# Two Swin blocks in one kernel: new orders of work on all five queues, a new ring of PSUM banks, and a semaphore step in place of a one-column product

## The reference

```
h = layernorm(x) * g + b                      # A0 / A1 in the kernel
h = roll(h, (-3, -3)); cut into windows of 7 x 7 = 49 tokens
q, k, v = h @ Wqkv + bqkv                     # first block 4 heads of 24, second 12 heads of 8
a = softmax(q * scale @ k.T + relative_bias[head] + shift_mask[window])
o = (a @ v) @ Wproj + bproj; windows back, rolled back
x = x + o
m = gelu(layernorm(x) @ W1 + b1)              # M0 / M1; hidden width 384
first block only: m = layernorm(m) * g3 + b3
x = x + m @ W2 + b2
```

## Time and profile before

| | us |
|---|---|
| median of 3 runs | 6845.63 |
| profiled execution, whole | 6848.46 |
| profiled execution, span from first to last instruction | 6846.5 |
| PE busy | 6637.3 (97%) |
| DVE busy | 5211.6 (76%) |
| ACT busy | 5460.3 (80%) |
| GpSimd (POOL) busy | 4494.8 (66%) |

### The profile page before, as it was taken

One profiled execution on the slowest core, in us unless ns is written; L12 is line 12 of the kernel. 1 busy time (PEld: TensorE's weight loads), 2 busy tenths in 40 slices (PEclk: granted clock), 3 DMA queues, 4 the chain that ended last, 5 costly groups with the idle time before them and its releaser, 6 DMA issues.

```text
span 6846.5 us, 283694 instructions
## 1 busy us (share of the span) xinstructions
PE 6637.3 (97%) x97324; PEld 5821.8 (85%) x97324; DVE 5211.6 (76%) x18725; ACT 5460.3 (80%) x11268; POOL 4494.8 (66%) x4612
## 2 busy tenths in 40 slices
PE   6999999999999999999999999999999999999998
PEld 5888888888888888888888888888888888888887
DVE  5777777777777777777777777777777777777775
ACT  4888888888888888888888888888888888888886
POOL 3666666666666666666666666666666666666664
PEclk8999999999999999999999999999999999999998
DMA  2111111111111111111111111111111111111111
GB/s 63 47 50 45 50 46 49 47 49 47 49 48 48 48 47 48 47 49 47 50 46 50 46 50 45 50 45 50 46 50 47 49 47 49 47 48 48 48 48 34
DMA packets 604527, 327.79 MB, mean 48 GB/s; under 512 B 449916, under 2 KB 603902, under 8 KB 604094
## 3 DMA queue, kind: packets, MB, share of 16 engines
q1 hardware_dynamic: 603992, 322.32, 18.2%
q10 hardware_dynamic: 486, 4.82, 0.2%
HBM read 82.89 MB, written 38.54 MB: 18 GB/s over the span
## 4 chain that ended last, share of the span: by engine, by line
PE 44%; SPq 39%; DMA 8%; issue 6%; ACT 2%; DVE 1%; POOL 0%; POOLq 0%; DVEq 0%; ACTq 0%
SPq L343 20%; PE ps L396 13%; SPq L331 10%; PE ps L486 10%; DMA vM<-vA 8%; PE ps L422 6%; PE ps L453 3%; SPq L321 3%; PE ps L510 3%; PE ps L432 3%; PE ps L414 3%; ACT kT L641 2%; SPq L313 2%; PE ps L523 2%; SPq L300 2%
## 5 line engine op out<-in xcount | busy, mean ns | idle before, releaser
L975 POOL TENSOR_TENSOR hid_sq<-hid 128x1176 f32<-128x1176 f32 x256 | 550.1, 2149 | 1443.2 <-ACT hid L696 1443.2
L679 ACT ACTIVATE probsT<-ps 98x392 f32<-98x392 f32 x2048 | 952.9, 492 | 498.9 <-PE ps L396 498.4
L848 DVE TENSOR_TENSOR shifted<-ps,negmax 113x392 f32<-113x392 f32 x2048 | 1161.3, 567 | 213.2 <-DVE negmax L844 0.5
L844 DVE TENSOR_REDUCE negmax<-ps 113x8 f32<-113x392 f32 x2048 | 1147.3, 560 | 208.8 <-PE ps L453 208.5
L396 PE MATMUL ps<-ident,probs 113*98 113x113 f32 x8192 | 1076.5, 264 | 9.5 <-ACT probs L672 5.8
L486 PE MATMUL ps<-vM,probsT 98*49 98x18 f32 (+1 forms) x32768 | 944.5, 202 | 134.1 <-DMA vM<-vA 132.4
L486 PEld LDWEIGHTS ps<-vM,probsT 98*49 98x49 f32 x32768 | 838.4, 125 | 272.6 <-issue 163.6
L672 ACT ACTIVATE probs<-shifted 113x392 f32<-113x392 f32 x2048 | 988.5, 518 | 9.8 <-DVE shifted L848 6.8
L664 ACT ACTIVATE ps<-table 113x392 f32 (+1 forms) x2048 | 956.4, 498 | 13.9 <-DVE y_out L880 2.6
L396 PEld LDWEIGHTS ps<-ident,probs 113*98 113x98 f32 x8192 | 801.0, 128 | 129.6 <-issue 81.1
L947 POOL TENSOR_TENSOR rstdA<-var_epsA,minus_half 98x4 f32<-98x4 f32 x512 | 517.4, 1011 | 576.5 <-DVE var_epsA L827 576.3
(11 more groups left out here) (98 smaller groups left out, 14713.8 us busy)
## 6 DMA issues: line engine op xcount, KB each, us to landing
kM<-kT SPq DMA_DIRECT2D x512, 85.8 KB
vM<-vA SPq DMA_DIRECT2D x1024, 41.3 KB
vM<-vA SPq DMA_DIRECT2D x1024, 38.3 KB
x_in<-in_x SPq DMA_DIRECT2D x256, 147.0 KB
x_again<-in_x SPq DMA_DIRECT2D x256, 147.0 KB
kM<-kT SPq DMA_DIRECT2D x1024, 36.8 KB
x_keep<-x_next SPq DMA_DIRECT2D x256, 147.0 KB
out_y<-y_out SPq DMA_DIRECT2D x256, 147.0 KB
```

What stands on the lines that cost most here:

```text
L679: act.activation(probsT[:, unit_buffer(L, u), :, :, :], free(ps[bank_of[f"T{L}{u}"]][0:PT, 0:1], (SP, 4), (64, 2), (1, TOK)), ACT.Copy).th ...
L844: dve.tensor_reduce(negmax[:, buf, :], s, AX.X, ALU.max, negate=True).then_inc(s_mx[L], 1)
L848: dve.tensor_tensor(shifted[0:SP, buf, :].rearrange("p (h k) -> p h k", k=TOK), s, free(negmax[:, buf, 0:1], (1, 8), (0, TOK)), ALU.add).t ...
```

## The change

All five orders, the lags and the banks are replaced, LAST goes from 5 to 6, and the one-column product becomes an increment of a new semaphore s_ready by PE's sequencer, which carries the same wait; nothing waits for s_ready. No other operation is added, removed or altered. The orders before are in the listing above; of the diff the new lines stand here.

```diff
-LAST = 5
+LAST = 6
...
+        s_ready = sem("s_ready")
...
+        BANKS = [("f1_1_1", 6, 0), ("k1", 4, 3), ("q1", 4, 1), ("xtM0", 3, 3), ("f1_2_1", 6, 0), ("v1", 4, 1),
+                 ("oT1", 5, 4), ("f1_0_0", 3, 3), ("f1_1_0", 3, 0), ("f1_2_0", 3, 4), ("pj1", 5, 1),
+                 ("xtA0", 1, 0), ("sc10", 4, 2), ("sc11", 4, 5), ("sc12", 4, 3), ("f2_1", 6, 1), ("T00", 2, 0),
+                 ("T01", 2, 4), ("f2_0", 3, 2), ("sc13", 4, 5), ("sc14", 4, 1), ("sc15", 4, 4), ("o0", 2, 7),
+                 ("T10", 4, 0), ("k0", 1, 3), ("T11", 4, 5), ("T12", 4, 0), ("q0", 1, 1), ("T13", 4, 3),
+                 ("oT0", 2, 5), ("v0", 1, 0), ("xtM1", 5, 3), ("pj0", 2, 2), ("o1", 4, 6), ("sc00", 1, 1),
+                 ("sc01", 1, 5), ("f1_0_1", 5, 0), ("xtA1", 3, 3), ("T14", 4, 4), ("T15", 4, 2)]
...
-                    pe.matmul(ps[bank_of["sc00"]][0:1, 0:1], ident[:, 1:2], ident[:, 0:1], start=False, stop=True, skip_group_check=True)
+                    pe.sem_inc(s_ready, 1)
```

More of the change, by code:

```diff
@@ L346, in body @@
             def body(i):
-                s0, s1, s2, s3, s5 = Strip(i, 0), Strip(i, 1), Strip(i, 2), Strip(i, 3), Strip(i, 5)
+                s0, s1, s4, s6 = Strip(i, 0), Strip(i, 1), Strip(i, 4), Strip(i, 6)
+                variants(s4, 1)
+                spread_v(s4, 1)
                 load(s0)
-                keep(s3)
+                store(s6)
+                keep(s4)
+                variants(s1, 0)
                 spread_v(s1, 0)
                 load_residual(s1)
[L352 to L355, removed]
             iterate(sp, body)
@@ L570, in body @@
[L570 to L598, removed]
+                s1, s2, s3, s4, s5, s6 = Strip(i, 1), Strip(i, 2), Strip(i, 3), Strip(i, 4), Strip(i, 5), Strip(i, 6)
@@ new lines, in body @@
+                fc1(s6, 1, 1)
+                k(s4, 1)
+                q(s4, 1)
+                attend(s5, 1, 4)
+                attend(s5, 1, 5)
+                xT(s3, "M0")
+                fc1(s6, 1, 2)
+                v(s4, 1)
+                o_turn(s5, 1)
+                fc1(s3, 0, 0)
+                fc1(s3, 0, 1)
+                fc1(s3, 0, 2)
+                project(s5, 1)
+                xT(s1, "A0")
+                scores(s4, 1, (0, 1, 2))
+                fc2(s6, 1)
+                probs_turn(s2, 0, 0)
@@ new lines, in body @@
+                probs_turn(s2, 0, 1)
+                fc2(s3, 0)
+                scores(s4, 1, (3, 4, 5))
+                attend(s2, 0, 0)
+                attend(s2, 0, 1)
+                probs_turn(s4, 1, 0)
+                k(s1, 0)
+                probs_turn(s4, 1, 1)
+                probs_turn(s4, 1, 2)
+                q(s1, 0)
+                probs_turn(s4, 1, 3)
+                o_turn(s2, 0)
+                v(s1, 0)
+                xT(s5, "M1")
+                project(s2, 0)
+                attend(s4, 1, 0)
@@ L600, in _ @@
+                attend(s4, 1, 1)
+                attend(s4, 1, 2)
+                attend(s4, 1, 3)
+                scores(s1, 0, (0, 1))
+                fc1(s5, 1, 0)
+                xT(s3, "A1")
+                probs_turn(s4, 1, 4)
+                probs_turn(s4, 1, 5)
             iterate(pe, body)
@@ new lines, in body @@
+                gelu(s6, 1, 0)
+                turned(s4, "A1")
+                probsT_out(s5, 1, 4)
+                probsT_out(s5, 1, 5)
+                seed(s4, 1, 0)
+                gelu(s6, 1, 1)
+                k_out(s4, 1)
+                q_out(s4, 1)
+                seed(s4, 1, 1)
+                turned(s3, "M0")
+                gelu(s6, 1, 2)
+                v_out(s4, 1)
+                o_out(s5, 1)
+                gelu(s3, 0, 0)
+                gelu(s3, 0, 1)
+                seed(s4, 1, 2)
@@ new lines, in body @@
+                gelu(s3, 0, 2)
+                exps(s2, 0, 0)
+                exps(s2, 0, 1)
+                turned(s1, "A0")
+                probsT_out(s2, 0, 0)
+                probsT_out(s2, 0, 1)
+                seed(s4, 1, 3)
+                exps(s4, 1, 0)
+                seed(s4, 1, 4)
+                seed(s4, 1, 5)
+                exps(s4, 1, 1)
+                exps(s4, 1, 2)
+                probsT_out(s4, 1, 0)
+                k_out(s1, 0)
+                exps(s4, 1, 3)
+                probsT_out(s4, 1, 1)
@@ L744, in _ @@
+                probsT_out(s4, 1, 2)
+                probsT_out(s4, 1, 3)
+                o_out(s2, 0)
+                exps(s4, 1, 4)
+                q_out(s1, 0)
+                turned(s5, "M1")
+                v_out(s1, 0)
+                seed(s1, 0, 0)
+                seed(s1, 0, 1)
+                exps(s4, 1, 5)
             iterate(act, body)
@@ L914, in body @@
             def body(i):
-                s0, s1, s2, s3, s4, s5 = Strip(i, 0), Strip(i, 1), Strip(i, 2), Strip(i, 3), Strip(i, 4), Strip(i, 5)
-                stats(s0, "A0")
[L917 to L936, removed]
+                s0, s1, s2, s3, s4, s5, s6 = Strip(i, 0), Strip(i, 1), Strip(i, 2), Strip(i, 3), Strip(i, 4), Strip(i, 5), Strip(i, 6)
+                normalise(s5, 1)
+                low_part(s3, 0)
+                residual(s5, 1)
+                shift(s4, 1, 0)
+                shift(s4, 1, 1)
+                finish1(s6)
+                shift(s4, 1, 2)
+                stats(s5, "M1")
+                third_stats(s3)
+                shift(s4, 1, 3)
+                shift(s4, 1, 4)
+                normalise(s2, 0)
+                finish0(s3)
+                stats(s3, "A1")
+                shift(s4, 1, 5)
+                residual(s2, 0)
+                low_part(s5, 1)
+                stats(s2, "M0")
+                shift(s1, 0, 0)
+                stats(s0, "A0")
+                shift(s1, 0, 1)
             iterate(dve, body)
```

64 lines of the change are left out of this document (11 added, 53 removed), and 6 rows, old and new, of the table BANKS.

## The result

The changed kernel took 6871.22 us (median of 7 runs, 6868.61 to 6876.12), the kernel before 6849.05 us beside it (7 runs, 6842.89 to 6854.27). The ratio is 1.0035 (95% interval 1.0026 to 1.0045): slower by 0.35%. I had predicted 6628 us, in a range of 6585 to 6740.

What follows compares the result with a forecast made beforehand. TensorE's own issue plus its wait for vM bounds the kernel; 26.22 - 0.73 - 0.06 - 0.16 + 0.10 = 25.37 us a strip, 0.85 less over 256 strips, gives 6628 us, 8-in-10 range 6585 to 6740.

Steps and rivals of the forecast that it cites:

- ACT's order: Turn of the loop: exps 5, table load, gelu and turned fit before k by 0.1 us plus the fc1.
- Rival 2: New wait replaces the old, likeliest at the loop's turn or sequencer's increment: 0.6 to 0.8 us a strip back; chance 0.10.
- vM, -0.73: SyncE's new order copies encoder 1's vM sooner, so TensorE's wait at L486 goes: -0.73 us a strip.
- The product of one column, -0.06: L445 on TensorE becomes a sequencer increment: -0.06 us a strip, between gain 0.12 and loss 0.09.
- Stretches, -0.16: TensorE has four stretches of small products a strip instead of five: -0.16 us, bounds -0.33 and +0.10.
- small waits, +0.10: Waits of the new order ending just before TensorE needs them; some come late: +0.10 us a strip (0 to 0.3).
- VectorE's order: L895 falls from 0.93 to 0.16 us, so q, reached at 3.59 us, does not wait for shift 4.
- rival 1: L895 stays at 0.93 us beside a GpSimd instruction and q waits 0.47 us: 6748 or 6723 us; chance 0.11.
- Rival 3: Ring through VectorE and the table load becomes the bound, slower than before, 6943 us at 26.6 a strip; chance 0.05.
- LAST = 6: Filling and emptying outside the ring: counted as 0 us, range -5 to +20 us.

Runs made afterwards that it cites:

- experiment 1: Changed kernel with gelu's two waits swapped (fc2's first, fc1's last): 6586.77 us, ratio 0.9622 to the kernel before.
- experiment 2: Changed kernel with gelu's two waits swapped only in the hardware loop, unrolled turns as they were: 6582.24 us, ratio 0.9616 to the kernel before.
- experiment 3: Kernel before with a semaphore step on ACT in encoder 1, putting the table load behind fc1's wait: 7192.49 us, ratio 1.0508.
- experiment 6: Kernel before, encoder 1's vM copies earlier on SyncE: one call moved, 8314.94 us; instead encoder 0's vM copies taken from in front, 6832.18 us.
- experiment 8: Kernel before with encoder 0's vM copies moved behind encoder 1's and add_bias moved behind rstd_of_third: 6662.64 us; with s_ready increment for one-column product too: 6661.65 us.
- experiment 4: Changed kernel with gelu's waits swapped and the old one-column product in place of the increment: 6622.16 us, ratio 0.967 to the kernel before.
- experiment 5: Kernel before with only the one-column product replaced by the semaphore increment: 6846.19 us, ratio 0.9998.
- experiment 7: Kernel before with add_bias(s4, 1) moved behind rstd_of_third(s2) on GpSimd, away from L895: 6845.38 us, ratio 0.9998.

## Why the prediction was wrong

The sum of what the change does to TensorE was nearly right: I had 25.37 us a strip, the kernel after without its hole takes 25.15 (experiment 1). The prediction failed in one step, and a rival that I gave 0.10 names its place. By the periods measured: -0.75 for vM and L895 together, -0.13 for the product, -0.22 for the rest of the order and +1.18 for the table load make +0.08 (26.25 to 26.33). The first of these was measured in the old order. I had -0.73, -0.06, -0.06 and nothing for the load.

**The step that failed** is ACT's order: "It fits, by 0.1 us plus the fc1, if exps 5 was done in time." Two things were wrong in it. First, it counted the load as done whenever the exponential is done and put nothing for it behind fc1; in the head of the loop the load waits for fc1, 1.60 us after the exponential is done, and that costs 1.18 us a strip (experiments 1 and 2; 3 shows the like in the other order). Secondly, it asked whether ACT is ready for k, while the first that wants ACT is fc1(s6, 1, 1), which takes gelu's bank, as the list of banks in the diff shows. This second point is the smaller: with another bank fc1 could have begun 0.92 us earlier and k have been wanted at 3025.54, but the copy turned(s4, "A1") ends only at 3026.14, so by these rows about 0.6 us would have stayed (an estimate; no run tried it). From the end of fc1(s5, 1, 0) TensorE has three turns to do, ACT the load of 1.28 us and gelu of 0.59. With the load out of the way the turns cover it, and ACT is even 0.23 us idle before gelu; with the load in it TensorE stands for 0.92 us, and the turns with the hole grow by 1.15. The kernel's text doesn't name the load; the trace does, and in the timeline before it could be seen that the load ran beside its fc1 and so that its place matters.

**Rival 2** had "most likely at the turn of the loop, where the branch, the table load and k meet", at 0.6 to 0.8 us a strip. The place was right, the price too low by a third to a half: 1.15 to 1.18. I priced it as margins overrun, not as a whole load of 1.28 moved onto the path.

**vM, -0.73.** The wait is gone, and its price was right as a price on TensorE (48 products now 1.21 us). But alone it is worth 0.07 (experiment 6); only with L895's fall is it worth 0.75 (experiment 8). The prediction took the whole -0.73 for the vM wait alone, and had L895's fall for another reason, so that the sum came out near is in part luck. It had the chain (q waits if L895 stays), in the new order; that the kernel before is bound by the same chain 0.07 us behind its vM wait I had not looked for.

**The product of one column, -0.06.** In the new order it is 0.13 (experiment 4), about the gain of 0.12 that I had as one bound: the increment hides wholly. In the old order it is 0 (experiment 5).

**Stretches, -0.16, and small waits, +0.10.** From the kernel before with its two chains mended (25.50) to the new order mended (25.15) it is 0.35 us; less the product's 0.13 the new order itself gives 0.22, where I had 0.06. How that divides between fewer stretches and waits that are no longer there, such as the one for low_part, was not tried.

**VectorE's order** came out as predicted: q doesn't wait (it starts 3.56 us after scores(s4, 1, (3, 4, 5)), from 3013.76 to 3017.32, where I had 3.59), and L896 is at 0.16. Here the Trainium skill (SBUF — State Buffer, section Who interferes with whom), by which any GpSimd instruction that reads SBUF shuts a VectorE instruction with two SBUF inputs out, would hold L896 until inverse_root ends, and so at 0.27 us in the row shown, and L895 of experiment 7 at 0.9. The trace agrees with that rule under the addition over 384 columns (0.93 us beside 1.00) and disagrees under inverse_root with four columns (0.16 beside 1.02, in all 252 runs of experiment 7 that start beside it); the measurement decides, and rival 1 was rightly priced low.

**Rival 3** didn't come: in the traces of the new order TensorE has no steady wait for VectorE. **LAST = 6**: outside the ring the kernel after spends 133 us, before 127, so +6, within what I gave; with the load in its place it is 140 to 148.

**The range** of 6585 to 6740 left out the whole of rival 2 and of anything slower. It would have held the time of the kernel with the load in its place (6587, and 6582 in its best form, just below). Most of the margins that I called small held; what moved the result was an instruction that I had not placed.

## What to carry to other kernels

When an order is turned so that another operation comes first in a loop's body, look at the instructions of the queue there and not at the text: a wait can sit on a register instruction, and an inserted table load then stands behind it. There is no one right order of the waits in the text: in the head of this loop fc1's wait had to be written last, in the unrolled turns first. So look, in each place, at which wait the load stands behind; here two waits swapped were worth 284 us of 6871. And where a wait that bounds a kernel is taken away, add up the second-longest chain to the same place first: two edits worth 14 us and nothing by themselves were worth 183 together.

## What the runs showed of the hardware

- A GpSimd instruction's length isn't what holds VectorE up. Two of nearly the same length differ: the addition over 384 columns (1.00 us) held L895 at 0.93, inverse_root over four columns (1.02 us) left it at 0.16, though GpSimd had begun first by 0.1 us both times. The two differ in operation and in columns; which of these counts was not tried.
- A semaphore increment in TensorE's order, ahead of small products and ended before the attends ahead of it had, cost nothing: with it the scores follow 64 attends after 1.58 us (3020.58 to 3022.16), and the period is 0.13 us shorter than with a product of one column in its place.
- A table load of 1.28 us was followed by its activation 1.30 us after the load began (3023.88 and 3025.18), so a change of table costs its load and little else, if the load is not made to wait.
- TensorE stood still for 3.06 us in experiment 6, and the granted clock was at 1.2 GHz from 0.21 us before it went on until 6.61 us after: the hole cost more than its length.
